# A kernel of two preactivated layers, capsules and windowed attention: one convolution for the last layer and its fold, early loads, and layer norm applied by the attention phase

## The reference

```python
x = x + _L0_conv_ref(_gn(x), L0_conv_weight)      # capsule convolution with 3 routing rounds
x = x + _L1_conv_ref(_gn(x), Wr, Wqkv, Wp, bp, W1, b1, W2, b2)

def _L1_conv_ref(x, Wr, Wqkv, Wp, bp, W1, b1, W2, b2):
    xp = jnp.pad(x, ((0, 0), (0, 0), (1, 1), (1, 1)))
    pat = jnp.stack([xp[:, :, i:i + H, j:j + W] for i in range(3) for j in range(3)], axis=2)
    t = pat.reshape(B, C * 9, H * W).transpose(0, 2, 1)
    t = t + _dmha(_ln2(t), Wr, Wqkv, Wp, bp)       # _ln2: mean and variance over a whole sample
    t = t + _mlp(_ln2(t), W1, b1, W2, b2)          # relu(t W1' + b1) W2' + b2, 288 -> 72 -> 288
    y = t.transpose(0, 2, 1).reshape(B, C, 9, H, W)
    out = jnp.zeros((B, C, H + 2, W + 2), x.dtype)
    # the nine taps (i, j) of y are added to out, each shifted by (i, j)
    return out[:, :, 1:H + 1, 1:W + 1]
```

## Time and profile before

| what | us |
| --- | --- |
| median of 3 runs (12758.24 to 12763.55) | 12761.37 |
| the profiled execution | 12757.43 |
| its span | 12755.6 |
| n1 | 0 to 79.5 |
| routing | 79.5 to 3992 |
| n2 | 3996.7 to 4209.2 |
| attention | 4209.2 to 11965.1 |
| last phase (fold) | 11965.1 to 12755.6 |
| in it: DVE's preparation ends / PE's first hide | 11985.96 / 11994.48 |

### The profile page before, as it was taken

One profiled execution on the slowest core, in us unless ns is written; L12 is line 12 of the kernel. 1 busy time (PEld: TensorE's weight loads), 2 busy tenths in 40 slices (PEclk: granted clock), 3 DMA queues, 4 the chain that ended last, 5 costly groups with the idle time before them and its releaser, 6 DMA issues. The chain is left out here.

```text
span 12755.6 us, 252307 instructions
## 1 busy us (share of the span) xinstructions
PE 12098.4 (95%) x71228; PEld 4438.5 (35%) x71228; DVE 8919.5 (70%) x16555; ACT 7556.9 (59%) x15286; POOL 3737.3 (29%) x3524
## 2 busy tenths in 40 slices
PE   6999999999995699999999999999999999999899
PEld 2333333333332233333333333333333333333233
DVE  6777777777776577777777777777777777777211
ACT  4666666666664266666666666666666666666411
POOL 4767777777773000000000000000000000000243
PEclk9999999999997699999999999999999999999999
DMA  3101101101013333333333333333333333333355
GB/s 79 23 16 23 23 16 23 22 16 23 16 23 108 92 75 80 87 76 76 87 77 78 84 82 76 83 83 75 81 85 76 77 87 76 77 85 76 79 120 110
DMA packets 957932, 843.94 MB, mean 66 GB/s; under 512 B 658772, under 2 KB 693172, under 8 KB 945332
## 3 DMA queue, kind: packets, MB, share of 16 engines
q1 hardware_dynamic: 955060, 818.75, 28.5%
q10 hardware_dynamic: 1536, 8.39, 0.3%
HBM read 577.74 MB, written 247.05 MB: 65 GB/s over the span
## 5 line engine op out<-in xcount | busy, mean ns | idle before, releaser
L1580 DVE TENSOR_REDUCE a_big<-a_mp 128x1 f32<-128x512 f32 x8192 | 5178.4, 683 | 1917.4 <-PE a_mp L1417 1911.7
L1503 ACT ACTIVATE a_ex<-a_sc 128x512 f32<-128x512 f32 x8192 | 4393.7, 601 | 1723.7 <-PE a_sc L1405 1719.7
L1417 PE MATMUL a_mp<-a_ks,a_qs 108*128 108x512 bf16 x8192 | 3129.8, 383 | 47.2 <-DMA a_ks<-qk_parts 26.3
L1405 PE MATMUL a_sc<-a_qs,a_ks 111*128 111x512 bf16 x8192 | 3123.6, 383 | 40.5 <-issue 30.2
L546 POOL TENSOR_TENSOR r_prod<-r_temp,r_win 128x512 f32<-128x512 f32 x1792 | 2095.6, 1189 | 1158.6 <-ACT r_temp L845 939.1
L893 DVE TENSOR_TENSOR r_prod<-r_pg,r_win 128x512 f32<-128x512 f32 x2816 | 1846.5, 683 | 784.5 <-PE r_pg L618 444.2
L1431 PE MATMUL a_po<-a_ex,a_va 128*32 128x512 f32 x16384 | 2217.0, 606 | 12.2 <-issue 10.8
L1405 PEld LDWEIGHTS a_sc<-a_qs,a_ks 111*128 111x128 bf16 x8192 | 795.5, 97 | 2587.8 <-ACT a_ex L1503 1735.6
L1325 POOL TENSOR_TENSOR a_on<-a_oc,a_zb 128x512 f32<-128x512 f32 x256 | 325.1, 1270 | 3505.1 <-DMA a_zb<-z_rows 3505.1
L1313 POOL TENSOR_TENSOR a_pieces<-a_left,a_pieces 128x512 bf16<-128x512 f32 x256 | 295.6, 1155 | 3323.9 <-ACT a_pieces L1489 3323.9
L1417 PEld LDWEIGHTS a_mp<-a_ks,a_qs 108*128 108x128 bf16 x8192 | 801.7, 98 | 983.1 <-DVE a_big L1580 300.5
(11 more groups left out here) (180 smaller groups left out, 11113.9 us busy)
## 6 DMA issues: line engine op xcount, KB each, us to landing
a_qs<-qk_parts SPq DMA_DIRECT2D x768, 144.0 KB
a_ks<-qk_parts SPq DMA_DIRECT2D x768, 144.0 KB
qk_parts<-a_pieces SPq DMA_DIRECT2D x128, 768.0 KB, 5.0
f_t<-mixed SPq DMA_DIRECT2D x48, 1536.0 KB, 16.4
a_tw<-second SPq DMA_DIRECT2D x512, 128.0 KB, 3.0
a_zb<-z_rows SPq DMA_DIRECT2D x256, 256.0 KB
mixed<-a_t SPq DMA_DIRECT2D x256, 256.0 KB, 5.5
r_win<-first SPq DMA_DIRECT2D x128, 280.5 KB, 5.0
```

The costliest lines, as they stand in the source:

```text
L1405: pe.matmul(sc[k % BANKS][:, :], ks[0:KROWS + NPART, p.h, head, 128 * kb:128 * kb + 128], qs[0:KROWS + NPART, p.h, head, CHUNK * qb:CHUNK ...
L1417: pe.matmul(mp[k % BANKS][:, :], qs[0:KROWS, p.h, head, 128 * q:128 * q + 128], ks[0:KROWS, p.h, head, CHUNK * half:CHUNK * half + CHUNK], ...
L1503: nc.scalar.activation(ex[:, k % RING, :], sc[k % BANKS][:, :], ACT.Exp, scale=scale).then_inc(exped.sem, 1)
L1580: nc.vector.tensor_reduce(big[:, x % 2, k // 2:k // 2 + 1], mp[k % BANKS][:, :], AX_X, ALU.max).then_inc(maxed.sem, 1)
```

## The change

**norm_phase.** All four tiles have buffers of their own in `raw` and `more`; SP issues all loads first and all stores behind them. n2 no longer has `count`, `weighted`, `squares`, `ln_pad`, and stores neither the layer-normed image nor the summed one. The sums for the layer norm come from the row's BN statistics (nine times) less the edges: ACT sums two edge rows, two edge columns and the corners, plain and squared (six small operations a tile), and DVE's `layer(t)`, 18 tiny operations, makes scale and shift of each row; it stands behind BN_STATS of tile t+1, and for the last tile at the end. `layered` now holds two numbers a row, stored at the end in eight DMAs.

**attention_phase.** `load_window` takes the group-normed image `second` and, in three more small DMAs, the scale and shift; POOL's `layer` applies them to the window at the start of a unit, and `qk` waits for that (`zw_ready`) and no longer for the load.

**fold_phase.** `unhide` and `u` are gone. `hidden` becomes a framed 66x66 image with two buffers, and `fold(q)` takes the nine taps of W2 from it straight into f_pf (36 matmuls of 32 output columns), and then the three column shifts of `three` (12). `f_ph` has four PSUM buffers. SP loads `t` of sample p+2 as soon as POOL's eighth sum of p is made, ahead of the store of p; the image comes as two transfers, `x` and the routed one (half a megabyte more in a sample), behind the store, and DVE adds them.

```diff
@@ norm_phase @@
-    raw = sb("raw", [128, 2, PIX])
...
+    raw = sb("raw", [128, tiles, PIX])
...
-            if t >= 2:
-                sp.wait_ge(images, t - 1)
-                if add is not None:
-                    sp.wait_ge(kept[t % 2], 16 * (t // 2))
-            sp.dma_start(raw[:, t % 2, :], src[128 * t:128 * t + 128, :]).then_inc(loaded[t % 2], 16)
+            sp.dma_start(raw[:, t, :], src[128 * t:128 * t + 128, :]).then_inc(loaded[t], 16)
...
+            sp.wait_ge(images, t + 1)
+            for s in range(4):
+                for h in range(2):
+                    r0 = h * LANES * CROWS
+                    rows_of = padded[C * s:C * s + C, t % 2, r0:r0 + HALF_ROWS, :]
+                    sp.dma_start(halves[8 * t + 2 * s + h, :, :],
+                                 rows_of.rearrange("p a b -> p (a b)")).then_inc(stored[t % 2], 16)
+        if n_ln:
+            sp.wait_ge(ln_known, tiles)
+            for t in range(tiles):
+                for h in range(2):
+                    sp.dma_start(ln_stats[8 * t + h:8 * t + 8:2, :, :], told[:, t, :]).then_inc(ln_kept, 16)
+            sp.wait_ge(ln_kept, 16 * 2 * tiles)
...
+                act.wait_ge(images, t + 1)
+                ends, inner = slice(1, IMG + 1, IMG - 1), slice(1, IMG + 1)
+                for k, (a, b) in enumerate(((ends, inner), (inner, ends), (ends, ends))):
+                    part = padded[:, t % 2, a, b]
+                    if k == 1:
+                        part = part.rearrange("p a b -> p b a")
+                    to = [edge[:, 2 * k + i, :, 0:part.shape[2]] for i in range(2)]
+                    nc.scalar.activation(to[0], part, ACT.Copy, accum_out=acc[:, 2 * k:2 * k + 1]).then_inc(acted, 1)
+                    nc.scalar.activation(to[1], part, ACT.Square, accum_out=acc[:, 2 * k + 1:2 * k + 2]).then_inc(acted, 1)
...
             link(last)
+            if n_ln and t:
+                layer(t - 1)
             nc.vector.bn_aggr(mv[:, :], stats[:, :, :].rearrange("p a b -> p (a b)")).then_inc(to_pe, 1)
...
@@ attention_phase @@
-            image = ln_halves[p.m, :, :].rearrange("c (a b) -> c a b", b=PAD)
+            image = halves[p.m, :, :].rearrange("c (a b) -> c a b", b=PAD)
             for j in range(3):
+                sp.dma_start(lnsc[C * j:C * j + C, p.h, :], ln_stats[p.m, :, :]).then_inc(zw_in[p.h].sem, 16)
...
+        def layer(p):
+
+            pool.wait_ge(zw_in[p.h].sem, zw_in[p.h].at(p.m, 96))
+            pool.sem_inc(zw_here, 1)
+            nc.gpsimd.tensor_scalar(zw[:, p.h, :], zw[:, p.h, :], lnsc[:, p.h, 0:1], lnsc[:, p.h, 1:2],
+                                    ALU.mult, ALU.add).then_inc(zw_ready.sem, 1)
...
+            if 2 in which:
+                layer(offset(p, 2))
...
-                    pe.wait_ge(zw_in[own.h].sem, zw_in[own.h].at(own.m, 48))
+                    pe.wait_ge(zw_ready.sem, zw_ready.at(own.n, 1))
@@ fold_phase @@
-                    store(Pass(2 * i + h, h, i))
+                    p = Pass(2 * i + h, h, i)
+                    sp.wait_ge(summed.sem, summed.at(p.n, CHUNKS))
                     load(Pass(2 * i + 2 + h, h, i + 1))
+                    store(p)
+                    load_image(Pass(2 * i + 2 + h, h, i + 1))
...
-        def unhide(p, k):
-
-            pe.wait_ge(h_done.sem, h_done.at(p.n, min(k + 2, CHUNKS)))
-            pe.wait_ge(u_done.sem, u_done.at(p.n, k - 1))
-            for i in range(3):
-                first = (CROWS * k + 2 - i) * IMG
-                last = pe.matmul(pw[k % 2][0:ROWS3, :], w2[:, i, :], hidden[:, first:first + CHUNK],
-                                 start=i == 0, stop=i == 2)
-            last.then_inc(w_made.sem, 1)
-
         def fold(p, q):
 
-            pe.wait_ge(u_done.sem, u_done.at(p.n, LANES * (q + 1)))
+            pe.wait_ge(h_done.sem, h_done.at(p.n, min(LANES * (q + 1) + 1, CHUNKS)))
+            pe.wait_ge(summed.sem, summed.at(p.n, LANES * (q + 1)))
             pe.wait_ge(out_done.sem, out_done.at(p.n, q - 1))
+            for j in range(3):
+                for i in range(3):
+                    for l in range(LANES):
+                        row = CROWS * (LANES * q + l) + 2 - i
+                        pe.matmul(pf[q][C * l:C * l + C, :].rearrange("p (a b) -> p a b", b=IMG), w2[:, i, C * j:C * j + C],
+                                  hidden[:, p.h, row:row + CROWS, 2 - j:2 - j + IMG], start=i == j == 0, stop=False,
+                                  tile_position=(0, C * l))
             for j in range(3):
                 for l in range(LANES):
                     last = pe.matmul(pf[q][C * l:C * l + C, :].rearrange("p (a b) -> p a b", b=IMG), sel[:, j, :],
-                                     u[:, LANES * q + l, :, 2 - j:2 - j + IMG], start=j == 0, stop=j == 2,
+                                     three[:, LANES * q + l, :, 2 - j:2 - j + IMG], start=False, stop=j == 2,
                                      tile_position=(0, C * l))
             last.then_inc(folded.sem, 1)
...
-            for k in range(CHUNKS + 2):
-                if k < CHUNKS:
-                    hide(p, k)
-                if k == 2 and not (isinstance(p.n, int) and p.n == 0):
+            for k in range(CHUNKS):
+                hide(p, k)
+                if k == 1 and not (isinstance(p.n, int) and p.n == 0):
                     fold(p.to(-1), 1)
-                if k == CHUNKS - 1:
+                if k == CHUNKS - 2:
                     fold(p, 0)
-                if k >= 2:
-                    unhide(p, k - 2)
...
-                pool.wait_ge(u_done.sem, u_done.at(p.n, k - 3))
-                nc.gpsimd.tensor_tensor(three[:, k % 4, :], two[:, :], t[:, p.h, 2, rows[2]],
+                pool.wait_ge(folded.sem, folded.at(p.n, k // LANES - 1))
+                if k == CHUNKS - 1:
+
+                    pool.wait_ge(h_made.sem, h_made.at(p.n, CHUNKS))
+                nc.gpsimd.tensor_tensor(three[:, k, :, 1:IMG + 1], two[:, :].rearrange("p (a b) -> p a b", b=IMG),
+                                        t[:, p.h, 2, rows[2]].rearrange("p (a b) -> p a b", b=IMG),
                                         ALU.add).then_inc(summed.sem, 1)
...
-            for k in range(CHUNKS):
-                dve.wait_ge(w_made.sem, w_made.at(p.n, k + 1))
-                dve.wait_ge(summed.sem, summed.at(p.n, k + 1))
-                if k % LANES == 0:
-
-                    dve.wait_ge(folded.sem, folded.at(p.n, k // LANES - 1))
-                nc.vector.tensor_tensor(u[:, k, :, 1:IMG + 1], pw[k % 2][0:ROWS3, :].rearrange("p (a b) -> p a b", b=IMG),
-                                        three[:, k % 4, :].rearrange("p (a b) -> p a b", b=IMG),
-                                        ALU.add).then_inc(u_done.sem, 1)
-                if k == 0 and not (isinstance(p.n, int) and p.n == 0):
-                    finish(p.to(-1), 1)
-                if k == CHUNKS - 2:
-                    finish(p, 0)
+            dve.wait_ge(x_in[p.h].sem, x_in[p.h].at(p.m, 128))
+            nc.vector.tensor_tensor(x1[:, p.h, :, :], x1[:, p.h, :, :], x2[:, p.h, :, :], ALU.add).then_inc(x_done.sem, 1)
+            if not (isinstance(p.n, int) and p.n == 0):
+                finish(p.to(-1), 1)
+            finish(p, 0)
```

More of the change, by code:

```diff
@@ L83, in sem @@
         return sems[-1]
-    raw = sb("raw", [128, 2, PIX])
-    more = sb("more", [128, 2, PIX]) if add is not None else None
+    raw = sb("raw", [128, tiles, PIX])
+    more = sb("more", [128, tiles, PIX]) if add is not None else None
     padded = sb("padded", [128, 2, PAD, PAD])
@@ L170, in _ @@
             pe.matmul(ps[:, 0:1], pairs[:, :], work[:, 1:2], start=True, stop=True).then_inc(avg, 1)
[L171 to L173 removed]
+        if n_ln:
+            layer(tiles - 1)
     @block.scalar
```

255 lines of the change are left out of this document (118 added, 137 removed).

## The result

The changed kernel takes 12566.51 us (median; 12564.89 to 12580.22, 4 runs) against 12761.43 before: a ratio of 0.9849, 95% interval 0.9837 to 0.9860. The prediction was 12571. The profiled execution has a span of 12564.8 us against 12755.6.

| phase | before | after | difference | predicted |
| --- | --- | --- | --- | --- |
| n1 | 79.49 | 67.61 | -11.9 | -11.7 |
| routing | 3917.22 | 3914.12 | -3.1 | 0 |
| n2 | 212.52 | 115.27 | -97.3 | -95 |
| attention | 7755.87 | 7762.83 | +7.0 | 0 |
| last phase | 790.5 | 705.0 | -85.5 | -83.4 |

The account below looks back on a forecast made before the run. Bounds by phase: DVE waits in the first normalisation, bytes in the second, TensorE in attention and the last phase. Terms -11.7 - 95 + 0 - 83.4 = -190 from 12757.4, plus 3.9 for the median: 12571 us, range 12535 to 12625.

Parts of the forecast that it names:

- n2: Second normalisation: fewer bytes and operations, DVE the bound at 20.8 us a tile; -95 us (-80 to -104).
- n1: First normalisation: all four tiles loaded at once, so DVE's waits for images go; -11.7 us (-9 to -12).
- last phase: Last phase: f_pw matmuls go, folds grow, a sample takes 41.9 us, 5.15 less; -83.4 us (-70 to -85).
- the tail of 13 us: First normalisation: 13.0 us from the last stores' issue to the next phase's first DMA stays, perhaps growing a little.
- Rival 3: Second normalisation ends late: tiny stores or their landing take 15 to 20 us more; 12590 us; chance 0.10.
- Rival 1: Last phase: long four-lane runs slower than short ones, sample 46.3 us, only 11 us gained; 12643 us; chance 0.10.
- 40 us for 24: Last phase: the early load of t has 40 us for the 24 it needs.
- rival 4: Last phase: fold waits for POOL's last sum or a late load, 3 to 5 us a sample; 12640; chance 0.05.
- the step on the operation's price: Attention: POOL's new operation on the window takes 2.9 us, or 1.4 if one input runs twice as fast.
- The term of 0: Attention: the new POOL operation and extra loads change the phase by 0 us (-10 to +18).
- Rival 2: Attention: POOL's operation holds the phase up, deciding at some 27 us in place of 3; 12827 us; chance 0.03.
- 24 us of room and takes 3: nothing: Attention, steady unit: POOL's operation takes 3 us within 24 us before PE needs the window, so costs nothing.

Follow-up runs that it names:

- Run 8: Changed kernel with two image buffers in both normalisations, loads of tiles 2 and 3 behind stores of tiles 0 and 1: 12593.00 us.
- runs 9 to 11: Changed kernel with statistics stored early (12566.92 us); then also the last phase's start trimmed (12558.53); then also both first t loads before both images (12556.04).
- run 2: Changed kernel with the last phase's load of t for sample p+2 behind the store of p: 12613.38 us.
- run 3: Changed kernel with the load of t behind the store, and PE and POOL waiting for the image too: 12707.71 us.
- Runs 7 and 4: Changed kernel with three (7) or eleven (4) more same-size POOL operations ahead of the one on attention's window: 12606.73 and 12665.09 us.
- run 6: Changed kernel with eleven more POOL operations behind the one on the window, on a tile of their own, PE not waiting: 12657.17 us.

## Why the prediction was right

**n1** (-11.7 / -11.9): the waits went and the tail of 13 us stayed. **n2** (-95 / -97.3): the form was right, DVE as the bound, one wait for landed stores (2.1 expected, 1.43 found), and the small DMAs at the end. The chain was sized at 5.0 and is 4.0 a tile; the first tile came 0.5 us later than I had it, and ACT's six sums over the edges take 2.0 us (1.99 at 4079.32) and not 2.7. Rival 3 is out: the small DMAs are issued in 6.13 us, and the next phase starts 5.0 later. Run 8 shows the split that the prediction only implied, and runs 9 to 11 that the small DMAs' issue is on the path: 2.3 us less of it at the end, n2 3 us shorter.

**The last phase** (-83.4 / -85.5): a pass was taken at 0.429 and is 0.431 in long runs, 41.86 a sample expected, 41.78 found. Rival 1 is out: four lanes do not slow in runs of 96. The price of the rival was too low by its own figures: 46.3 a sample leaves out the 0.32 us that the forecast has for a fold's gap; with it the sample is 46.9, and none of the 82 us would stay. The Trainium skill, TensorE: Matmul & The Clock Gate, Part 3, says that weight loads overlap running matmuls only in other row groups. The trace disagrees: with one row group PE is busy for all of the 23.46 us of the window above, and 7.20 us of weight loads lie within them. The table there, three column tiles at 2.38 of 3, would have given a pass of 0.54 us (an estimate); 0.431 was measured. The start gave 3.0 and not 2.4; the last fold waits 1.53 us (1.5 expected), for POOL's last sum, as said. That t has "40 us for 24" was right, and runs 2 and 3 show how much hung on it: rival 4 was priced at 3 to 5 us a sample, and a real lateness costs 3.4 (run 2) to 9.2 (run 3), since in these runs PE's waits were followed by a lower clock, and a later sample start sent the next load later.

**Attention** (0 / +7.0): the step on the operation's price was off, 2.9 us taken where 1.30 was measured, just below the lower bound of 1.4, without effect. The term of 0, though, is not quite right, and 7 us alone could not tell. With the same attention instructions the phase took 7762.8, 7754.5, 7768.9, 7766.0, 7775.2, 7757.7 and 7768.3 us (mean 7764.8), and with those of before 7755.9 and 7755.8. The steady part tells more: the last 59 of the 63 steps from one `a_packed` to the next sum to 6995.5 us in both executions with the instructions of before, and to 7004.8 to 7017.8 in the seven with the new ones. It is the long unit that grew: 119.81 us in the mean with the old instructions, in both executions, its shortest 118.34; 120.07 to 120.58 in the seven, their shortest 119.58. So the new instructions cost attention's steady part 9 to 22 us. Whether POOL's operation, the three small DMAs or the later gate of `qk` does it, no run shows; DVE's chain is not slower (0.19 us an operation).

**Where the reasoning was wrong.** Rival 2 was said to decide from an operation of some 27 us, because I looked only at who waits for it; the step "24 us of room and takes 3: nothing" left out what else runs at that time. Runs 7 and 4 show that POOL costs attention 44 us with 5.4 us of work and about 100 with 16, and run 6 that it does so without any gate: DVE's chain of small operations lies 4.8 us behind `a_on`, and the real operation ends just before it (5929.60, chain at 5931.51). That the change cost nothing there was luck: the chain starts 1.9 us later here, and 0.8 to 2.3 in the other steady units. The Trainium skill, SBUF — State Buffer, Who interferes with whom, says that the port pair shared by DVE and GpSimd is an exclusive lock, and that a DVE instruction with two SBUF inputs contends with a GpSimd instruction that reads SBUF. The trace agrees for `a_mleft` and the last `a_mparts`: 1.09 us in place of 0.19, each ended 0.04 us behind a POOL operation. In run 7 a CAST with one input was held as well (1.02 us), for which two inputs can't be the reason.
